# First attention: probabilities split into fp16 halves before they are turned, and three turned banks copied by two engines

## The reference, cut to what matters

```python
q_r = jnp.einsum('bshq,hqr->bhsr', q_big, W_qr)
k_r = jnp.einsum('bld,hdr->bhlr', kv_rope, W_kr)
scores = jnp.einsum('bhsr,bhlr->bhsl', q_r, k_r)
attn = jax.nn.softmax(scores, axis=-1)
ctx_c = jnp.einsum('bhsl,bld->bhsd', attn, kv_rope)
ctx_lat = jnp.einsum('bhsd,hkd->bshk', ctx_c, w_kc_kv)
out = ctx_lat.reshape(b, s, H * K) @ Wo.T
```

## Time and profile before

| | us |
|---|---|
| median of 3 runs | 1847.28 (1844.83 to 1847.87) |
| the profiled execution | 1844.54 |
| its span | 1842.9 |
| mean granted TensorE clock, share of 2.4 GHz | 0.931 |
| TensorE busy in the span | 1606.8 (87%) |
| VectorE busy | 1192.0 (65%) |
| ScalarE busy | 1036.1 (56%) |
| GpSimd busy | 611.1 (33%) |

### The profile page before, as it was taken

The page is one execution under the profiler, slowest core; times in us unless marked ns, Lnnn a source line. Parts: engine busy times, 40 slices in busy tenths (PEclk is TensorE's granted clock), DMA queues, the critical chain, the costliest instruction groups (busy, mean ns, idle before and its releaser), DMA issues. The chain is left out here.

```text
span 1842.9 us, 35610 instructions
## 1 busy us (share of the span) xinstructions
PE 1606.8 (87%) x11911; PEld 998.5 (54%) x11911; DVE 1192.0 (65%) x2678; ACT 1036.1 (56%) x2563; POOL 611.1 (33%) x481
## 2 busy tenths in 40 slices
PE   4788999999999979989997777784599999999993
PEld 3655656656656545555554454553466666666661
DVE  4866797787787779688796777757633333333332
ACT  3447746746747627566574777743655555455451
POOL 4614304304304300000000222212167777777662
PEclk9789999999999989999998998776599999999996
DMA  8820120220120249787786001104356656556536
GB/s 271 285 84 9 55 75 9 62 68 10 65 65 10 69 157 333 239 280 241 227 260 227 12 2 37 36 29 114 78 108 140 150 136 140 137 129 136 131 74 225
DMA packets 143332, 226.57 MB, mean 123 GB/s; under 512 B 37857, under 2 KB 93409, under 8 KB 143032
## 3 DMA queue, kind: packets, MB, share of 16 engines
q1 hardware_dynamic: 107160, 195.90, 33.6%
q0 software_dynamic: 29344, 21.29, 7.1%
q10 hardware_dynamic: 6656, 7.11, 1.1%
HBM read 175.00 MB, written 98.80 MB: 149 GB/s over the span
## 5 line engine op out<-in xcount | busy, mean ns | idle before, releaser
L2751 PE MATMUL g_ps<-ring,xT 128*128 x1572 | 300.8, 327 | 1.1 <-issue 1.1
L1051 POOL TENSOR_TENSOR pr<-pr,sm 128x1444 f32<-128x1444 f32 (+1 forms) x64 | 137.3, 2145 | 385.9 <-DVE sm L1087 385.9
L2700 POOL DMA_INDIRECT acc<-rows,slot_sources x131 | 207.8, 1586 | 107.2 <-issue 78.7
L2857 DVE SCALAR_TENSOR_TENSOR hf<-sg,g_ps 128x192 f32<-128x192 f32 x131 | 46.4, 354 | 238.5 <-ACT sg L2806 206.3
L2751 PEld LDWEIGHTS g_ps<-ring,xT 128*128 128x128 f16 x1572 | 142.8, 98 | 71.9 <-issue 5.5
L2690 POOL DMA_INDIRECT xg<-xtab,slot_sources x131 | 138.0, 1054 | 81.3 <-issue 79.5
L2773 PE MATMUL d_ps<-ring,hT 128*128 x655 | 162.8, 379 | 1.6 <-ACT hT L2819 1.1
L1081 DVE TENSOR_REDUCE sm<-s_banks 128x2 f32<-128x722 f32 (+2 forms) x128 | 97.5, 762 | 67.3 <-PE s_banks L819 64.8
L973 ACT ACTIVATE pr<-s_banks,sm 128x361 f32<-128x361 f32 (+1 forms) x208 | 115.3, 563 | 30.7 <-DVE sm L1081 29.2
L876 PE MATMUL o_bank<-cT,N_hi 128*128 128x400 f16 x512 | 129.7, 335 | 0.0
L819 PE MATMUL s_banks<-kvp,qp 128*128 128x361 f16 (+1 forms) x624 | 116.9, 318 | 10.8 <-ACT pr L973 6.1
(11 more groups left out here) (322 smaller groups left out, 3848.1 us busy)
## 6 DMA issues: line engine op xcount, KB each, us to landing
split_f<-in_gu SPq DMA_DIRECT2D x64, 384.0 KB, 4.5
split_gu<-split_o SPq DMA_DIRECT2D x64, 384.0 KB, 3.1
ring<-split_gu SPq DMA_DIRECT2D x32, 768.0 KB
head<-in_head SPq DMA_DIRECT2D x16, 864.0 KB
tern_w<-in_tern SPq DMA_DIRECT2D x48, 256.0 KB
split_f<-in_down SPq DMA_DIRECT2D x32, 384.0 KB, 4.2
split_d<-split_o SPq DMA_DIRECT2D x32, 384.0 KB, 3.8
ring<-split_d SPq DMA_DIRECT2D x32, 256.0 KB
```

The source lines that it names most:

```text
L1051: nc.gpsimd.tensor_tensor(pr[:, s % 3, 0:n], pr[:, s % 3, 0:n], small[:, s % 3, 2, 0:n].unsqueeze(2).to_broadcast([P, n, KEYS]), ALU.mult) ...
L2700: nc.gpsimd.indirect_dma_start(out=core.acc[i % NACC][:, :], out_offset=bass.IndirectOffsetOnAxis(ap=core.sources[:, i:i + 1], axis=0), in ...
L2751: last = nc.tensor.matmul(g_ps[i % 2][:, 0:2 * INTER], xT[:, i % 2, a * KT + k, :], ring(i, (2 * k + w) * 2 * INTER, 2 * INTER), start=((k ...
```

## The change

The probabilities are split before the turn, and turned as fp16:

- GpSimd's scaling of a step is two instructions, one for each part e.
- ScalarE (new probs_hi) rounds the scaled part to fp16 in SBUF (ph, 722 or 361 columns); VectorE (new probs_lo) subtracts it from the scaled fp32 part and writes the lower half to ph. "parted" counts the lower halves.
- TensorE turns each tile twice for each block, the upper and the lower half, with an fp16 identity, into a bank read as fp16 of 2 x 512 columns. Turn 0 waits for both lower halves of its step.
- Copies of both halves at once from the banks to pT: banks 0 and 1 by ScalarE (probs_out), bank 2 by VectorE (probs_out, p_free2).
- pr has two buffers in place of three, split in two tensors; exponentials e0 wait for the lower halves of the step two earlier. The Ternary buffers are separate tensors in a new order over pr and ph, and waits of loads and of rounding follow it.
- The fp16 identity lies in ident_b, which ScalarE writes before and restores after the stage.

The core of the diff:

```diff
@@ turn (TensorE)
-                        pe.wait_ge(weighed.sem, weighed.after(c * STEPS + s))
+                        pe.wait_ge(parted.sem, parted.after(c * STEPS + s))
...
                     for i, n in tiles_of(s % GROUPS):
-                        last = nc.tensor.transpose(pb[u][0:KEYT[u], i * P:i * P + n],
-                                                   pr[0:n, s % 3, i, u * P:u * P + KEYT[u]],
-                                                   core.ident[0:n, 0:n])
+                        for a in range(2):
+                            last = nc.tensor.transpose(pb[u][0:KEYT[u], a, i * P:i * P + n],
+                                                       ph[s % 2][0:n, a, i, u * P:u * P + KEYT[u]], ident_h[0:n, 0:n])
                     last.then_inc(p_turned.sem, 1)
@@ ScalarE
+                    if e == 0 and c * STEPS + s >= 2:
+                        act.wait_ge(parted.sem, parted.after(c * STEPS + s - 2))
...
-                def probs_hi(c, s, u):
+                def probs_out(c, s, u):
                     act.wait_ge(p_turned.sem, p_turned.after(c * STEPS + s, u + 1))
                     n = width(s)
-                    nc.scalar.activation(pT[s % 2][0:KEYT[u], 0, u, 0:n], pb[u][0:KEYT[u], 0:n], ACT.Copy
-                                         ).then_inc(p_hi.sem, 1)
+                    nc.scalar.activation(pT[s % 2][0:KEYT[u], :, u, 0:n], pb[u][0:KEYT[u], :, 0:n], ACT.Copy
+                                         ).then_inc(p_free.sem, 1)
+
+                def probs_hi(c, s):
+                    if c * STEPS + s >= 2:
+                        act.wait_ge(p_turned.sem, p_turned.after(c * STEPS + s - 2))
...
+                    for e in range(2):
+                        n, at = half_of(s, e)
+                        act.wait_ge(normal.sem, normal.after(c * STEPS + s, e + 1))
+                        nc.scalar.activation(ph[s % 2][0:n, 0, at, 0:KEYS], pr[s % 2][0:n, at, :], ACT.Copy
+                                             ).then_inc(tile_hi.sem, 1)
@@ ScalarE, order in iteration s
                             exps(c, s - 1, 1)
...
-                        if 2 <= s < STEPS + 2:
-                            probs_hi(c, s - 2, 0)
-                            probs_hi(c, s - 2, 1)
...
+                        if 2 <= s < STEPS + 2:
+                            probs_out(c, s - 2, 0)
                         if s < STEPS:
                             exps(c, s, 0)
+                        if 2 <= s < STEPS + 2:
+                            probs_out(c, s - 2, 1)
+                        if 1 <= s < STEPS + 1:
+                            probs_hi(c, s - 1)
                         if s >= 3:
                             context_hi(c, s - 3)
-                        if 2 <= s < STEPS + 2:
-                            probs_hi(c, s - 2, 2)
@@ GpSimd
+                    for e in range(2):
+                        n, at = half_of(s, e)
+                        probs, scale = pr[s % 2][0:n, at, :], small[0:n, s % 3, 2, at]
+                        nc.gpsimd.tensor_tensor(probs, probs, scale.unsqueeze(2).to_broadcast([n, at.stop - at.start, KEYS]),
+                                                ALU.mult).then_inc(normal.sem, 1)
@@ VectorE
+                def probs_lo(c, s, e):
+                    n, at = half_of(s, e)
+                    dve.wait_ge(tile_hi.sem, tile_hi.after(c * STEPS + s, e + 1))
+                    nc.vector.tensor_tensor(ph[s % 2][0:n, 1, at, 0:KEYS], pr[s % 2][0:n, at, :],
+                                            ph[s % 2][0:n, 0, at, 0:KEYS], ALU.subtract).then_inc(parted.sem, 1)
+
+                def probs_out(c, s):
+                    dve.wait_ge(p_turned.sem, p_turned.after(c * STEPS + s))
                     n = width(s)
+                    nc.vector.tensor_copy(pT[s % 2][0:KEYT[2], :, 2, 0:n], pb[2][0:KEYT[2], :, 0:n]).then_inc(p_free2.sem, 1)
@@ VectorE, order in iteration s
-                        if 2 <= s < STEPS + 2:
-                            probs_lo(c, s - 2, 0)
                         if 1 <= s < STEPS + 1:
                             invert(c, s - 1)
-                        if 2 <= s < STEPS + 2:
-                            probs_lo(c, s - 2, 1)
...
                             peaks(c, s, 1)
                         if s >= 3:
                             context_lo(c, s - 3)
+                        if 1 <= s < STEPS + 1:
+                            probs_lo(c, s - 1, 0)
                         if 2 <= s < STEPS + 2:
-                            probs_lo(c, s - 2, 2)
+                            probs_out(c, s - 2)
+                        if 1 <= s < STEPS + 1:
+                            probs_lo(c, s - 1, 1)
```

More of the change, by code:

```diff
@@ L601, in __init__ @@
         self.o = [None] * D
[L602 to L609, removed]
+        self.s, self.m, self.a, self.g, self.w = ([None] * D for _ in range(5))
+        for part, k in TERN_ORDER:
+            {"s": self.s, "m": self.m, "a": self.a, "g": self.g, "w": self.w, "o": self.o}[part][k] = core.sb(
+                ctx, f"tern_{part}{k}", [P, DIM], F32 if part == "w" else BF16)
         self.bytes = D * DIM * (5 * 2 + 4)
@@ L631, in spread_sums @@
         pe.wait_ge(self.rounded.sem, self.rounded.after(n, 1))
-        self.nc.tensor.matmul(bank, self.core.gsum[:, :], self.a[:, k, :], start=True, stop=True
+        self.nc.tensor.matmul(bank, self.core.gsum[:, :], self.a[k][:, :], start=True, stop=True
                               ).then_inc(self.spread.sem, 1)
@@ L696, in attention0 @@
         oT = core.sb(ctx, "oT", [P, 2, CH], F32)
+        ident_h = core.ident_b[:, :].bitcast(F16)
         with ExitStack() as shared:
             tern = Ternary(core, shared)
-        pad = tern.bytes // (3 * 4 * 4)
-        assert pad >= KEYS and STEPS % 3 == 1
-        pr = core.sb(ctx, "pr", [P, 3, 4, pad], F32)[:, :, :, 0:KEYS]
+        assert STEPS % 2 == 0
+        pr = [core.sb(ctx, f"probs{p}", [P, widest, KEYS], F32) for p, widest in enumerate((4, 3))]
+        ph = [core.sb(ctx, f"probs_parts{p}", [P, 2, widest, ROW_PAD], F16) for p, widest in enumerate((4, 3))]
+        core.sb(ctx, "tern_end", [P, tern.bytes // 4 - sum(w * (KEYS + ROW_PAD) + 8 for w in (4, 3))], F32)
         sbank = ctx.enter_context(nc.psum_tensor("s_banks", [P, 4, 512], F32))
@@ L704, in attention0 @@
         ob = core.banks(ctx, "o_bank", 2)
-        pb = (tb[0], tb[1], ob[0])
+        pb = [bank[:, :].bitcast(F16).rearrange("p (a n) -> p a n", a=2) for bank in (tb[0], tb[1], ob[0])]
         def q_bank(c, hp):
@@ L726, in width, with half_of @@
             return r.stop - r.start
+        def half_of(s, e):
+            tiles = halves(s, e)
+            return tiles[0][1], slice(tiles[0][0], tiles[-1][0] + 1)
         def halves(s, e):
@@ L757, in _ @@
                     keys_in(c * CB + 3)
-                    sp.wait_ge(p_free.sem, p_free.after(c * STEPS + STEPS - 3))
+                    sp.wait_ge(parted.sem, parted.after(c * STEPS + STEPS - 2))
                     for u in range(2 * D):
+                        if u == D - 1:
+                            sp.wait_ge(p_turned.sem, p_turned.after(c * STEPS + STEPS - 2))
                         tern.load(sp, *place_of(c, u), w_ternary)
@@ L951, in _ @@
             def _(act):
+                nc.scalar.activation(ident_h, core.ident[:, :], ACT.Copy)
                 tern.rounded.start(act)
@@ L995, in round_off @@
                     for u in units:
+                        if u == 0:
+                            act.wait_ge(p_turned.sem, p_turned.after(c * STEPS + STEPS - 2))
+                        if u == D - 1:
+                            act.wait_ge(parted.sem, parted.after(c * STEPS + STEPS - 1))
                         tern.round_off(act, *place_of(c, u))
@@ L1044, in _ @@
                             copy_out(c, m)
+                act.wait_ge(p_turned.sem, p_turned.after(NCH * STEPS - 1))
+                nc.scalar.activation(core.ident_b[:, :], core.ident[:, :], ACT.Copy)
             @block.gpsimd
@@ L1108, in ternary @@
                     for u in units:
+                        if u == 0:
+                            dve.wait_ge(parted.sem, parted.after(c * STEPS + STEPS - 1))
                         tern.ternary(dve, *place_of(c, u), sums_at(u))
```

38 lines of the change are left out of this document (19 added, 19 removed).

## The result

The changed kernel takes 2038.4 us (median of 4, 2035.2 to 2042.3), against 1846.1 of the kernel before in the same runs: a ratio of 1.1046, 95% interval 1.1019 to 1.1073. It is slower by 193 us; 2028 were forecast. In this part "ratio" is always to the kernel before on the same chip, and a difference of ratios is turned into us with 1846. Medians leave out one execution of e1, which took 2437 us at a mean granted clock of 0.65 where the others of e1 had 0.91 to 0.92; the trace of e1 is of that one, so no rows of e1 are shown.

A forecast was written before the change was run, and what follows sets the result against it. TensorE bounds the steps before, at 4.50 us; afterwards a queue-order chain does, at 7.3. Own time 1844.5 + 163 + 18 for the clock = 2025.5, plus 2.7 to the median: 2028 us, range 1985 to 2105.

The forecast's parts named there:

- The ring: First attention: chain through ScalarE, VectorE and TensorE queues sets the period, 29.2 us in four steps, 7.3 a step.
- The fp16 copy from PSUM: VectorE's copies of turned bank 2: 0.55 us for 768 columns, 0.48 for 640, going by a row of 1024.
- The upper bound of 1.3 us in four steps: VectorE's bank copies at 1.01 ns a column, as for fp32: 1.3 us more in four steps, 18 in all.
- The clock: TensorE idling in the first attention starts cold, about +0.7 us in each of 25 of 56 periods: +18.
- After step 14 "nothing, except in the last chunk": After step 14, queries and values keep TensorE busy about 7 us, covering 5.4; only the last chunk costs +2.
- 14 periods: First bank copy of step 0 to step 14: 13 x 7.3 plus 6.3, 101.2 us a chunk, +152 altogether.
- The start of a chunk: Longer scalings, halves and turns put the first bank copy about 1.7 us later in each chunk: +7.
- Behind the last bank copy: Everything outside the first attention was to stay unchanged: 0 in the sum.
- Faster: First attention stays TensorE-bound and only its wait for GpSimd goes: -17, 1830 us; chance 0.04.
- ScalarE's amount alone: Queues decouple and ScalarE's 19.2 us replaces 18.0 in four steps: +17, +7 at the starts, 1871 us; chance 0.08.
- A cold clock throughout: All first-attention periods run with a cold TensorE, some 8.9 us each: +90, 2100 us; chance 0.12.

The follow-up runs named there:

- e1: Changed kernel with VectorE's context lower half issued behind both lower halves instead of ahead of them: 1966.7 us, ratio 1.0636.
- e2: Changed kernel with VectorE's context lower half behind both lower halves and its bank 2 copy ahead of them: 1943.4 us, ratio 1.0523.
- e5: Changed kernel with an extra 722-column ScalarE copy in 48 iterations, placed ahead of the context copy: 2068.2 us, ratio 1.1217.
- e4: Changed kernel with an extra 722-column ScalarE copy in 48 iterations, placed behind the second exponentials: 2041.2 us, ratio 1.1041.
- e6: Changed kernel with 12 extra matmuls filling TensorE's idle time ahead of turn 0: 2022.2 us, ratio 1.0959.
- e9: Changed kernel with 12 extra matmuls ahead of turn 0 and ScalarE's next-chunk query copies behind the bank copies: 2015.9 us, ratio 1.0911.

## Why the prediction was right

- **The ring** was the cause: e1 and e2 shorten it by order alone, e5 lengthens it, and e4 puts the same work beside it. Its sum of 29.2 us in four steps stands against 29.3 measured with the clock held (e6). The terms: bank copies on ScalarE 0.813 (0.81 taken), upper halves 0.821 (0.80), lower halves 0.919 (0.89), the fp16 bank copy on VectorE 0.549 (0.55), scalings 1.391 (1.39).
- **The fp16 copy from PSUM** went by the row of 1024 columns, not by the rule of one element a cycle in the Trainium skill, VectorE: DVE Perf Modes, "Rules for kernel authors". The measured 0.549 us for 768 columns decides for the row; at 1.01 ns a column, as for fp32 in the earlier trace rows, it would have been 0.94. The upper bound of 1.3 us in four steps was added up too low: with 1.20, 0.94, 0.94 and 0.81 for the four widths it is 1.6, or 22 in all. The forecast doesn't use it.
- **The clock** was priced at +18; holding it gives 16 back (e6). The trace shows 7 of these in steps 0 to 13 (387.3 against 379.9 us), where I had put nearly all of the 18, and 5 in step 13 to 14. Of the 56 periods counted, 18 hold a fall of the clock, not 25, and the 15 falls in steps 0 to 13 cost 0.5 each, not 0.7. Of all that I put into the sum this was the least founded, and its agreement is luck: without it steps 0 to 13 were put at +142, and the clock's 7 make that 149 of the 151.5 measured.
- **After step 14 "nothing, except in the last chunk"** failed, with "14 periods" for step 13 to 14: those two stretches took 33 us where the sum had 14. The step looked only at TensorE, which has work there. It passed over that the diff moves ScalarE's query copy ahead of the bank copy, so that the turned bank waits for a product of another chunk. In step 13 to 14 the traces put 5.0 us on the clock (e6) and 8.3 on this order (e9), of which 7.6 came back behind it. What makes up the rest of the 19, in step 14 to 15 above all, no experiment takes apart. That the total came out within 10 us of the forecast is luck too: these 19 too little stand against some 9 too much in steps 0 to 13.
- **The start of a chunk** was put at +7 and is +3.4. The first bank copy comes at 147.2 to 151.6 us in the nine traces of changed kernels other than e1, so of its first part (-0.3 for +1.7) nothing can be said; the cause of the rest wasn't looked for.
- **Behind the last bank copy** the trace after is 5.9 us longer. In the second trace of the changed kernel (after_again, span 2027.9) that stretch is 1215.0, as in the kernel before, so the 5.9 is spread between executions and the 0 of the sum holds.
- **The rivals.** Faster and ScalarE's amount alone were refuted by the period of 7.5; by e4 even 34 us more of ScalarE cost nothing that can be measured. A cold clock throughout: the granted clock of four steps was 0.89, not 0.50.

## What to carry to other kernels

Where several engines hand work round through queues that run in order, write for each iteration the closed chains (instruction, what it waits for, what stands ahead of it in its queue, back to the same instruction one iteration later) and sum each: the longest is the period, whatever the busy shares say. A new stage that needs two more handovers lengthens such a chain by everything that stands between its instructions in the queues, here 2.8 us a step (4.5 to 7.3) for work that, by ScalarE's amount of 19.2 us in four steps, would have cost 0.3 by my estimate. And when one ring is shortened, price the next longest before you count the gain; and read a diff for every instruction that an edit moves, the neighbours' too.

## What the runs showed of the hardware

TensorE with 12 useless matmuls a step made the kernel 16 us faster (e6). Without them TensorE stands idle for 1.4 to 3.6 us in each step ahead of turn 0, and the granted clock fell 15 times in steps 0 to 13 to the 1.2 GHz level, for about 3 us each; with the gaps filled it stayed at 1.00 there. One such fall: TensorE was busy 1.95 of the 4.4 us from 196.0 to 200.4 at 0.98, then 3.28 of 3.30 at 0.50, and behind them the clock was back at 1.00. An fp16 source gives ScalarE nothing (0.813 us for 768 columns, 0.85 ns a column as for fp32), while VectorE copies as many fp16 columns from PSUM in 0.549.
